# Splitting GpSimd's subtraction of the row maxima into two halves, with one scatter behind each, in the first attention of a two-layer gated block

## The reference

```python
x = x + tanh(g_xattn[0]) * attention(layernorm(x), ctx, ctx, mask, Wq, bq, Wk, bk, Wv, bv, Wo, bo)
    # logits = q k^T / sqrt(8) - mask * FMAX;  w = softmax(logits);  o = w v;  o Wo + bo
x = x + tanh(g_ffn[0]) * experts(layernorm(x), router_w, w_fc, b_fc, w_proj, b_proj)
    # probs = softmax(x router_w^T); the 2 largest, renormalised; gelu(x w_fc + b_fc) w_proj + b_proj
x = x + tanh(g_xattn[1]) * attention1(layernorm(x), ctx, ctx, ...)
x = x + tanh(g_ffn[1]) * quantised_ffn(layernorm(x), ...)
```

## Time and profile before

| | |
|---|---|
| median of 3 executions | 895.19 us (894.82 to 900.1) |
| profiled execution: span of the core | 960.7 us (no other time of it is given) |
| TensorE busy / VectorE / ScalarE / GpSimd | 746.5 / 742.0 / 612.7 / 594.2 us |
| mean granted clock of TensorE | 0.895 of full speed |
| first attention | about 15 to 400 us, 64 tiles |
| experts, with the rest of the scatters | about 400 to 740 us |
| second attention and feed-forward | about 740 to 960 us |

### The profile page before, as it was taken

One profiled execution on the slowest core, in us unless ns is written; L12 is line 12 of the kernel. 1 busy time (PEld: TensorE's weight loads), 2 busy tenths in 40 slices (PEclk: granted clock), 3 DMA queues, 4 the chain that ended last, 5 costly groups with the idle time before them and its releaser, 6 DMA issues. The chain is left out here.

```text
span 960.7 us, 19492 instructions
## 1 busy us (share of the span) xinstructions
PE 746.5 (78%) x6609; PEld 573.8 (60%) x6612; DVE 742.0 (77%) x1800; ACT 612.7 (64%) x1222; POOL 594.2 (62%) x571
## 2 busy tenths in 40 slices
PE   4898788988888888788698888999963889256255
PEld 2666577666666667666576766777751667122144
DVE  5999987877777887568566666777844799799998
ACT  5666556757576664567366656666753878399493
POOL 4675377777777777564556566665665983388600
PEclk9999989999999999899798999999985999676556
DMA  9327222222223123646476566575627832000023
GB/s 246 101 78 128 86 73 101 82 101 78 100 80 111 47 93 123 214 140 204 150 260 217 193 239 216 208 259 202 222 93 239 273 110 78 14 0 1 0 66 111
DMA packets 88625, 128.20 MB, mean 133 GB/s; under 512 B 19392, under 2 KB 62352, under 8 KB 82512
## 3 DMA queue, kind: packets, MB, share of 16 engines
q1 hardware_dynamic: 78528, 107.63, 34.6%
q0 software_dynamic: 9120, 18.91, 5.6%
q10 hardware_dynamic: 880, 0.43, 0.2%
HBM read 82.66 MB, written 44.18 MB: 132 GB/s over the span
## 5 line engine op out<-in xcount | busy, mean ns | idle before, releaser
L491 POOL DMA_INDIRECT m_results<-a_probs,e_to x156 | 161.6, 1036 | 94.5 <-issue 50.2
L500 POOL TENSOR_TENSOR a_probs<-a_probs,a_top 128x1024 f32<-128x1024 f32 x64 | 122.0, 1907 | 91.5 <-DVE a_top L1425 90.6
L481 POOL DMA_INDIRECT m_tokens_to<-r_rows,r_place x128 | 131.3, 1026 | 53.3 <-issue 31.0
L710 ACT ACTIVATE room<-a_ps_s,e_bias 128x512 f32<-128x512 f32 x156 | 107.3, 697 | 79.5 <-PE a_ps_s L1007 64.6
L1452 DVE CAST e_hp<-room 128x512 fp32r<-128x512 f32 x156 | 70.1, 449 | 82.8 <-ACT room L710 30.9
L618 ACT ACTIVATE a_probs_t<-a_ps_pt 128x512 f32<-128x512 f32 x128 | 70.1, 592 | 94.3 <-PE a_ps_pt L913 91.2
L1454 DVE TENSOR_TENSOR e_hp<-room,e_hp 128x512 fp32r<-128x512 f32 x156 | 109.9, 705 | 5.4
L1390 DVE TENSOR_TENSOR a_probs<-a_ps_s,a_mask 128x1024 f32<-128x1024 f32 x64 | 77.9, 1217 | 16.0 <-PE a_ps_s L798 11.5
L897 PEld LDWEIGHTS a_ps_o<-a_vals,a_probs_t 128*64 128x64 f32 x2048 | 68.1, 140 | 26.0 <-issue 25.2
L897 PE MATMUL a_ps_o<-a_vals,a_probs_t 128*64 128x18 f32 x2048 | 75.7, 214 | 4.8 <-issue 4.6
L1425 DVE TENSOR_REDUCE a_top<-a_probs 128x16 f32<-128x1024 f32 x64 | 77.2, 1206 | 0.2
(11 more groups left out here) (334 smaller groups left out, 2012.9 us busy)
## 6 DMA issues: line engine op xcount, KB each, us to landing
e_weights<-m_weights_to SPq DMA_DIRECT2D x39, 1024.0 KB
room<-m_tokens_to SPq DMA_DIRECT2D x39, 264.0 KB
m_weights_to<-r_parts SPq DMA_DIRECT2D x8, 1024.0 KB
c_two<-m_results SPq DMA_DIRECT2D x3, 1536.0 KB, 11.8
a_ctx_in<-in_ctx_dram SPq DMA_DIRECT2D x17, 256.0 KB, 3.5
m_keys_t<-n_keys SPq DMA_DIRECT2D x16, 256.0 KB
m_values<-n_values SPq DMA_DIRECT2D x16, 256.0 KB
out_dram<-x_sb SPq DMA_DIRECT2D x15, 256.0 KB, 2.3
```

The source lines that it names most:

```text
L481: pool.indirect_dma_start(tokens_to, bass.IndirectOffsetOnAxis(ap=place[:, k, q:q + 1], axis=0), rows[:, c % RING, q % CT, k, :], None).th ...
L491: pool.indirect_dma_start(results, bass.IndirectOffsetOnAxis(ap=to[:, v, r:r + 1], axis=0), y[:, v, r], None).then_inc(returned[v], 16)
L500: pool.tensor_tensor(probs[:, j], probs[:, j], top[:, j].unsqueeze(2).broadcast_to([P, HEADS, SEQ]), ALU.subtract).then_inc(shifted, 1)
L710: act.activation(h[:, c], ps_h[c], ACT.Gelu_apprx_tanh, bias=bias[:, n % ROWS, c:c + 1]).then_inc(h_sb, 1)
```

## The change

GpSimd's subtraction of one tile is written as two instructions of eight heads each (`shift(j, h)`), 128x512, and each raises `shifted` by one. The first of the tile's two scatters (`send_rows_of(t - 18, 0)`) is issued between the halves, and the second (`send_rows_of(t - 18, 1)`) stays where both stood, behind the powers and the renumbering. The waits at the start of a chunk come with the first scatter. TensorE waits for the first half ahead of the first four transposes and for the second half ahead of the second four. In the first 18 slots, where nothing is sent, the halves follow each other directly. After the loop both scatters are issued together as before.

```diff
-        def send_rows(q):
+        def send_rows_of(q, k):
             c = q // CT
-            if q % CT == 0:
+            if q % CT == 0 and k == 0:
                 pool.wait_ge(row_ready, CT * c + CT)
                 pool.wait_ge(placed, PLACE_OPS * c + PLACE_OPS)
                 pool.wait_ge(gate_set, GATE_OPS * c + GATE_OPS)
                 pool.wait_ge(ids, 4 + max(0, c - RING + 1))
+            beside_products()
+            pool.indirect_dma_start(
+                tokens_to, bass.IndirectOffsetOnAxis(ap=place[:, k, q:q + 1], axis=0),
+                rows[:, c % RING, q % CT, k, :], None).then_inc(sent[c % RING], 16)
+
+        def send_rows(q):
             for k in range(2):
-                beside_products()
-                pool.indirect_dma_start(
-                    tokens_to, bass.IndirectOffsetOnAxis(ap=place[:, k, q:q + 1], axis=0),
-                    rows[:, c % RING, q % CT, k, :], None).then_inc(sent[c % RING], 16)
+                send_rows_of(q, k)
+
+        def shift(j, h):
+            some = slice(HEADS // 2 * h, HEADS // 2 * h + HEADS // 2)
+            pool.tensor_tensor(probs[:, j, some], probs[:, j, some],
+                               top[:, j, some].unsqueeze(2).broadcast_to([P, HEADS // 2, SEQ]),
+                               ALU.subtract).then_inc(shifted, 1)
...
                 pool.wait_ge(top_ready, t + 1)
-                pool.tensor_tensor(probs[:, j], probs[:, j], top[:, j].unsqueeze(2).broadcast_to([P, HEADS, SEQ]),
-                                   ALU.subtract).then_inc(shifted, 1)
+                shift(j, 0)
+                if t >= SCATTER_LAG:
+                    send_rows_of(t - SCATTER_LAG, 0)
+                shift(j, 1)
                 if j == 0 and m >= 0:
                     powers(m)
...
                 if t >= SCATTER_LAG:
-                    send_rows(t - SCATTER_LAG)
+                    send_rows_of(t - SCATTER_LAG, 1)
...
         def probs_transposes(t):
-            pe.wait_ge(shifted, t - 1)
             if t - 2 >= 1:
                 pe.wait_ge(pt_sb, t * 2 - 4)
             for h in range(2):
+                pe.wait_ge(shifted, (t - 2) * 2 + 1 + h)
                 for k in range(4):
```

## The result

The changed kernel takes 918.7 us (median of 4 executions, 916.89 to 920.84) against 896.28 for the kernel before (4 executions beside it, 894.82 to 900.1): a ratio of 1.023 with an interval of 1.019 to 1.028. The forecast said 906 and a range up to 914: it had the direction right, and 11 us where 22 were measured.

The account below looks back on a forecast made before the run. It took VectorE and TensorE handing each other results as the bound, with GpSimd touching the loop only at the powers. Terms 6.7 + 0.2 + 0.2 + 3.1 + 0.8 + 0 = 11.0 us on 895.2 gave 906, range 896 to 914.

Parts of the forecast that it names:

- The powers 1.34 us later: GpSimd's powers, queued behind the j = 0 subtraction in groups 5 to 15; odd groups 5 to 13 add 6.7 us.
- the lock: VectorE operations reading two SBUF tensors are held until a GpSimd half ends; scan 3.1 us, table of tiles 0.8.
- Even groups 6 to 14 ... 0.2 us in all: Late powers at VectorE's line 1278 in even groups: nearly all covered by VectorE's slack, 0.2 us left.
- many short two-input operations ran beside the power operation unharmed: Argument for the rival that only the powers count (902.3 us, chance 0.26): VectorE's two-input operations need not be held.
- The cover: Even groups: VectorE's 0.28 us before line 1278 plus its 0.93 to 1.19 us wait for scores absorb the powers' delay.
- 1.34 - 1.17 = 0.2 us: Group 15: VectorE waits 1.17 us for scores, so only 0.2 us of the powers' delay is added.
- the clock: Rival, chance 0.12: more TensorE idle time brings a low-clock stretch in each odd group, 1.5 us each, 7.5 more, 913.
- The scan, 3.1: VectorE's line 1208 at j = 1 of five even groups, held by the second half: 3.1 us, bounds 0 and 5.2.
- The table of tiles, 0.8: Group 13: the table is worked out beside tile 53's second half and held once, 0.8 us, bounds 0 and 2.
- The offsets, "I take 0": VectorE's line 1152 in groups 1 to 4, held by the whole subtraction before: taken as 0, bounds -3.4 and +0.8 us.
- Executions without the profiler are 65 us shorter, and I can't see where: Caveat on the profiled span of 960.7 us against the median of 895.19, in the argument whether line 1390 has slack.
- not slower: Rival, chance 0.13: line 1390's wait for scores in odd groups swallows the delay, early offsets gain 3.4 us, 891.8.

Follow-up runs that it names:

- e1: The kernel before, unedited, profiled once more on chip 13: 900.53 us, ratio 1.001.
- e13: Changed kernel with the scatter between the halves in odd groups only, on chip 4: 970.19 us, ratio 1.010 to the kernel before.
- e5: Changed kernel with VectorE's offsets moved behind the maxima, on chip 15: 946.99 us, ratio 0.992 to the kernel before.
- e10: Changed kernel with VectorE's offsets moved behind the maxima, on chip 2: 942.93 us, ratio 0.984 to the kernel before.
- e4: Changed kernel with the scatter between the halves only at j = 0, the first tile of each group: 919.53 us, ratio 1.020 to the kernel before.
- e9: Changed kernel, unaltered, on chip 2 of the slower sort: 958.29 us, ratio 0.998 to the kernel before.
- e3: Changed kernel without the scatter between the halves at j = 0, the first tile of each group: 907.38 us, ratio 1.009 to the kernel before.
- e7: Changed kernel with the powers ahead of the first half at j = 0, on chip 15: 946.68 us, ratio 0.989 to the kernel before.

## Why the prediction was wrong

**Right.** A half at 1.04 us (1.046). The powers 1.34 us later, all of it added in the tight odd groups (1.36 each). That their sum fits, 6.9 forecast and 6.8 measured, is luck in part: group 5 didn't pay at j = 1 (0.06), and group 15 paid 1.36 where 0.2 was expected. VectorE's wait for them about 14 us, longest 2.6 (13.7, 2.6). That the lock exists and reaches the scan. That TensorE never waits for the subtraction itself. The expert part unchanged.

**The step that failed first** is "Even groups 6 to 14 ... 0.2 us in all": 6.5 us measured. I asked only when the powers would be ready, and compared that with VectorE's arrival at line 1278. I laid the second half of the tile with j = 1 over VectorE's two-input operations (the scan), but not that of the tile with j = 0, and `second_choice` begins just as that subtraction ends. The second half runs from 2.21 to 3.26 us after the subtraction's start (157.68, 159.89 to 160.94). `second_choice` starts 1.84 us after it (159.52; in e1 164.66 - 162.82, the same). By the starts on record its first operation (0.21 us) would have got through by 0.16 us, and the third (line 1181, two SBUF inputs, 2.34 to 2.57 us after the subtraction's start in e1) would have been held for some 0.7 us: 3.5 us in all, which could have been read from the trace of before. It came to 1.30 each because already the first is held. My sentence "many short two-input operations ran beside the power operation unharmed" hid this: they ran beside the powers then, and lie beside a subtraction now. e13 shows it (0.28 us and 24.8 for the slots without the scatter in between), and e5 that the powers aren't it. Over all places the forecast gave the holds 3.9 us (the scan and the table of tiles), and they took 11.

The cover that I had put against this, 0.93 to 1.19 us of waiting for scores, didn't help either: it stands in the profile of the slower sort of chip, and in e1 it is absent in these slots. The same holds for group 15, "1.34 - 1.17 = 0.2 us": 1.36 measured.

**The second** is the clock, which I had as a rival at 0.12 and not in the sum. Its price of about 1.5 us for a stretch was right (1.47, 1.55, 1.58), and with 1.3 us more idle time of TensorE one more such stretch costs time in three of five odd groups. But it comes two slots later than I looked, by way of TensorE's wait for line 1298, which shares a PSUM buffer with the transposes and stands behind VectorE's wait. In e5 and e10 the wait and the low clock go together. That the one brings the other is argued from this and from the order of events; no run changes the clock alone, and in group 7 of e4 and of e9 the same delay brings no low clock.

**Mis-sized terms.** The scan, 3.1: 1.65 measured, because VectorE comes 1.3 us later and because on the quick chips the whole subtraction already held it (0.47 to 0.72 in e1, 0.92 to 0.94 after; at my profile's 0.29 it was not held). The table of tiles, 0.8: 1.6, of which 1.3 are the cast with one input that my list of two-input operations left out. The offsets, "I take 0": four places of -0.6 to -0.9 (-0.86, -0.60, -0.59, -0.86), near the bound of -3.4, since VectorE does get both in at the boundary. The last weight split, in group 14, wasn't in the list: it starts beside the scatter, and is held until the second half is over.

```profile
363.85 2.51 DVE L1304 TENSOR_TENSOR r_parts<-r_raw,r_parts 128x1024 fp32r<-128x1024 f32 x1
```

```profile
363.20 0.99 POOL L480 DMA_INDIRECT m_tokens_to<-r_rows,r_place  x1 [0.16 <-ACT r_rows L642]
364.22 1.05 POOL L490 TENSOR_TENSOR a_probs<-a_probs,a_top 128x512 f32<-128x512 f32 x1
```

**The carried-over profile.** "Executions without the profiler are 65 us shorter, and I can't see where" was a wrong reading: the profiler has no part in it (e1 was profiled at 900.3). All 34 executions of the kernel before on chip 13 took 894 to 905 us and all 76 on chips 2, 4 and 15 took 948 to 978, so the forecast's profile most likely came from another chip than the times beside it; the record doesn't name it. The rival "not slower", 0.13, fits that sort of chip (0.998 in e9), though not by its mechanism: line 1390's wait for scores in odd groups doesn't swallow the delay (34.3 on both), the waits for TensorE at j = 0 vanish instead.

**A version that beats both** is the changed kernel with the offsets behind the maxima: 0.984 to 0.992 on three chips of the slower sort. On a chip of the quick sort it wasn't run. Its attention ends at 369 to 377 us on the slow sort, where the kernel before ends at 369.6 on the quick one, so there I would expect a draw at best.

## What to carry to other kernels

Moving a GpSimd operation by a microsecond is a change to VectorE: lay the new GpSimd intervals over VectorE's operations with two SBUF inputs and over its copies, casts and operations with a scalar on one, for the whole loop and not only where a semaphore joins the two, and charge each hit until the GpSimd operation ends. When a wait grows, follow everything behind the waiting instruction to the next engine, and ask of TensorE not only how long it idles but what the granted clock is in the products that come next. Check the span of the profiled execution against the timed median before a slack of one microsecond in it is called a cover; here 7% between them went with other slack.

## What was unexpected of the hardware

**An operation is held by a GpSimd operation that, by its record, has not begun.** In the changed kernel the held operation starts at 159.52, the half at 159.89, and beside it stands only the scatter (158.88 to 159.86). In e3 a copy starts at 257.74, 0.55 us before the half at 258.29, and in e7 line 1195 starts 0.73 us before its half. The scan 0.87 us before it (257.42 in e3) passes, and so does line 1325 0.77 us before a half in group 13 of e3 (0.16 us). Beside a scatter with no half close behind, a scan reads 0.29 us (e4), so the scatter isn't the one that holds. The Trainium skill, "SBUF — State Buffer", Who interferes with whom, says that whoever issues first gets the shared ports for the whole instruction; by the recorded starts VectorE was first in all three cases and waited all the same. One reading is that a GpSimd operation behind a scatter has its claim in before its record begins; no run tests that. For a forecast it's enough to begin the interval of such an operation 0.75 us early, an estimate between the 0.73 that was held and the 0.77 that passed.

**A copy is held too.** The 128x8 copy of e3 has one SBUF input, and takes 1.57 to 1.64 us instead of 0.17; the 1x13 cast of group 13 takes 1.45 instead of 0.14. The Trainium skill, "SBUF — State Buffer", Who interferes with whom, counts copies, casts and `tensor_scalar` among the operations that can take both ports; the trace agrees. A copy out of PSUM (line 1213, 0.20 us from 0.5 us before a half) and the reduction of the maxima (1.20 from 0.37 before one) aren't held. So it isn't enough to look for two inputs, and the forecast's profile already had the sign, one input, held beside a subtraction that starts at 120.21:

```profile
120.30 1.91 DVE L1140 TENSOR_SCALAR mean<-mean 128x8 f32<-128x8 f32 x1
```

**The same instructions, two sorts of chip.** 894 to 905 us or 948 to 978 for the kernel before, and the ratio of one change 1.023 or 0.998. Each chip was used in one session, so chip and session can't be told apart. Part of it sits in the attention's slots with j = 0 (+15 us), more in the experts: from 400 to 600 us TensorE is busy 168 us in the profile of the forecast and 191 in e1, with 196 against 245 GB/s moved. Why that is stays open.
